# Top-k attention masks: one GpSimd pass per tile with byte output, in place of a split between VectorE and a two-pass GpSimd form

## The reference, cut to what matters

```python
q, kk, v = (proj(wq), proj(wk), proj(wv))           # 8 images x 8 heads, 3136 tokens, 8 values a head
scores = jnp.einsum('bhqd,bhkd->bhqk', q, kk) * scale
vals, idx = jax.lax.top_k(scores, k)                # k = 32 of 3136
w = jax.nn.softmax(vals, axis=-1)
vg = jnp.take_along_axis(v[:, :, None, :, :], idx[..., None], axis=3)
out = jnp.einsum('bhqk,bhqkd->bhqd', w, vg)
```

## Time and profile before

| | us |
|---|---|
| median of 3 runs | 40168.95 |
| lowest, highest | 40162.17, 40170.39 |
| the profiled execution | 40166.83 |
| its span, first to last instruction | 40165.2 |
| outside the span | 1.6 |

### The profile page before, as it was taken

One profiled execution on the slowest core, in us unless ns is written; L12 is line 12 of the kernel. 1 busy time (PEld: TensorE's weight loads), 2 busy tenths in 40 slices (PEclk: granted clock), 3 DMA queues, 4 the chain that ended last, 5 costly groups with the idle time before them and its releaser, 6 DMA issues. The chain is left out here.

```text
span 40165.2 us, 616606 instructions
## 1 busy us (share of the span) xinstructions
PE 27334.3 (68%) x190808; PEld 12487.9 (31%) x190809; DVE 34028.5 (85%) x144824; ACT 21387.4 (53%) x28193; POOL 23707.4 (59%) x9390
## 2 busy tenths in 40 slices
PE   4557676666767667767347677777776777674399
PEld 4533332222333323333123233333332333331122
DVE  5659999999999999999669999999999999996611
ACT  1126665555666656656146566666665666663111
POOL 0017776666867667867037677777776777773000
PEclk7778888888888888888578788888888888886555
DMA  0010000000000000000110000000000000001100
GB/s 36 8 51 5 5 5 5 4 4 4 5 5 5 5 4 5 5 5 5 51 50 5 4 5 5 5 5 5 5 5 4 5 5 5 4 5 42 55 10 6
DMA packets 133141, 454.41 MB, mean 11 GB/s; under 512 B 29244, under 2 KB 85444, under 8 KB 111240
## 3 DMA queue, kind: packets, MB, share of 16 engines
q1 hardware_dynamic: 129256, 410.72, 3.0%
HBM read 244.71 MB, written 165.93 MB: 10 GB/s over the span
## 5 line engine op out<-in xcount | busy, mean ns | idle before, releaser
L225 POOL TENSOR_SCALAR B<-S,M 128x3136 bf16<-128x3136 f32 (+1 forms) x1920 | 15768.6, 8213 | 7934.6 <-DVE M L525 7848.3
L493 DVE MAX8 C<-S 128x8 f32<-128x112 f32 x89600 | 18738.3, 263 | 1002.3 <-issue 751.5
L418 ACT COPY S<-banks 128x896 f32<-128x896 f32 (+1 forms) x12800 | 10210.9, 815 | 8585.1 <-DVE C L493 3667.1
L439 ACT ACTIVATE W<-banks 128x1024 f32<-128x1024 f32 (+1 forms) x9524 | 9735.7, 1023 | 2747.3 <-PE banks L333 2696.0
L324 PE MATMUL banks<-Q,K 99*128 99x512 bf16 (+2 forms) x22550 | 6836.4, 390 | 3341.2 <-ACT S L418 2742.3
L286 PE MATMUL banks<-K,Q 96*128 96x448 bf16 x22400 | 6852.1, 385 | 3128.3 <-ACT S L418 2747.0
L230 POOL CAST Z<-B 128x3136 fp8e4<-128x3136 bf16 (+1 forms) x1920 | 6704.5, 3492 | 380.9 <-PE banks L333 136.4
L333 PEld LDWEIGHTS banks<-NEG,Z 128*128 128x128 fp8e4 (+1 forms) x80450 | 5968.7, 105 | 2753.9 <-issue 823.1
L333 PE MATMUL banks<-NEG,Z 128*128 128x128 bf16 (+3 forms) x80450 | 6817.7, 230 | 0.0
L369 PE MATMUL banks<-W,V 128*32 128x512 f32 (+1 forms) x45100 | 6726.3, 577 | 109.2 <-ACT W L442 79.0
L535 DVE TENSOR_SCALAR Z<-S,M 128x3136 fp8e4<-128x3136 f32 x1280 | 6033.2, 4713 | 369.7 <-PE banks L333 369.6
(11 more groups left out here) (200 smaller groups left out, 21899.3 us busy)
## 6 DMA issues: line engine op xcount, KB each, us to landing
q<-ln_o SPq DMA_DIRECT2D x20, 1568.0 KB, 5.1
ln_x<-y SPq DMA_DIRECT2D x16, 1568.0 KB, 6.0
K<-k_parts SPq DMA_DIRECT2D x130, 147.0 KB
Q<-q_parts SPq DMA_DIRECT2D x130, 147.0 KB
q_parts<-pj_parts SPq DMA_DIRECT2D x24, 784.0 KB, 4.7
k_parts<-pj_parts SPq DMA_DIRECT2D x24, 784.0 KB, 7.8
V<-v_rows SPq DMA_DIRECT2D x130, 112.5 KB, 7.4
v_rows<-pj_vt SPq DMA_DIRECT2D x8, 1800.0 KB, 11.2
```

What stands on the lines that cost most here:

```text
L225: chained(lambda: pool.tensor_scalar(m.B[0:rows, :], m.S[0:rows, slot(tile), :], m.M8[0:rows, side(i), t, 31:32], None, ALU.is_lt))
L418: act.copy(m.S[0:rows, slot(tile), at:at + CW * w].rearrange("p (a n) -> p a n", a=w), m.AB[0:rows, pair(score_at[a]):pair(score_at[a]) + ...
L439: ins = act.activation(m.W[:, e % 4, 0:n_banks, :], m.AB[:, b:b + n_banks, :], ACT.Exp)
L493: ins = dve.max(m.C[0:rows, tile % 2, TOP_AT + k:RANKED:CHUNKS], m.S[0:rows, slot(tile), CHUNK * k:CHUNK * k + CHUNK])
```

## The change

All ten entries of `MAKERS` become P, so VectorE makes no masks. GpSimd makes each in one instruction, which has two arithmetic steps in place of one: compare, then multiply by `ONE` = 56.0. The output is written as unsigned bytes into `Z`: 56 is the bit pattern 0x38, which is 1.0 when TensorE reads the byte as `float8e4`. The scratch `B`, the cast, and the waits that tied the two passes and consecutive masks together go. The wait for the mask slot (`e_mm`), which stood between the passes, now stands ahead of the only one.

```diff
-MAKERS = "DPPDPDPPDP"
+MAKERS = "PPPPPPPPPP"
+ONE = 56.0
@@
                 pool.wait_ge(found, tile + 1)
-                masks_done = sum(maker(x) == "P" for x in range(tile))
-                if masks_done:
-                    pool.wait_ge(z_pool, masks_done)
-                chained(lambda: pool.tensor_scalar(m.B[0:rows, :], m.S[0:rows, slot(tile), :],
-                                                   m.M8[0:rows, side(i), t, 31:32], None, ALU.is_lt))
                 if mask_freed(tile):
                     pool.wait_ge(e_mm, mask_freed(tile))
-                pool.wait_ge(part, parts[0])
-                pool.tensor_copy(mask_at(tile)[0:rows, :], m.B[0:rows, :], saturate=False).then_inc(z_pool, 1)
+                pool.tensor_scalar(mask_at(tile)[0:rows, :].bitcast(U8), m.S[0:rows, slot(tile), :],
+                                   m.M8[0:rows, side(i), t, 31:32], ONE, ALU.is_lt, ALU.mult).then_inc(z_pool, 1)
```

More of the change, by code:

```diff
@@ L7 @@
 FP8 = mybir.dt.float8e4
+U8 = mybir.dt.uint8
 I32 = mybir.dt.int32
@@ L609, in attend_memory @@
             ("V1", [128, 2, NT, 32], F32), ("S", [128, RING, TOK], F32), ("Z", [128, MASKS - MAKERS.count("A"), TOK], FP8),
-            ("B", [128, TOK], BF16), ("W", [128, 4, 2, QW], F32), ("O4", [128, QW], F32), ("OS", [HD + 1, 2, QW], F32),
+            ("W", [128, 4, 2, QW], F32), ("O4", [128, QW], F32), ("OS", [HD + 1, 2, QW], F32),
             ("C", [128, 2, RANKED], F32), ("C8", [128, NT], F32), ("M8", [128, 2, NT, 32], F32),
```

## The result

| | before | after |
|---|---|---|
| median of 4 runs (us) | 40169.67 | 46847.24 |
| lowest, highest | 40162.17, 40172.84 | 46837.19, 46849.31 |
| the profiled execution, its span | 40166.83, 40165.2 | 46846.82, 46845.2 |

What follows compares the result with a forecast made beforehand. VectorE bounds the kernel now, GpSimd after the change. Attention goes from 32,125 to 27,672 + 286 (block turns) + 2309 (searches) = 30,267 us; with 14 more saved, 1872 off 40,166.8 gives 38,295 us, range 37,400 to 47,050.

Steps and rivals of the forecast that it cites:

- the first term of the sum: GpSimd's mask passes in attention: 3200 at 8.21 us; with small work 8.65 us a tile, 27,672 us for 128 heads.
- three units: GpSimd's old comparison: 2.548 ns an element, a unit being the plain pass's 0.8365 ns, or 2.62 us for 3136 elements.
- the searches: GpSimd standing while VectorE searches in attention: 23 us on 90 occasions plus 239 us for second searches, 2309 us together.
- groups of short work: GpSimd's shift instructions, seven groups a head, each 1.51 us from its start to the next mask, 10.6 us a head.
- the moved wait: GpSimd's wait for TensorE to free a mask slot, now ahead of the pass; cost at nothing with 23 us of cover.
- its pace without masks: VectorE in attention without its masks and the waits ahead of them: 9.115 - 2.07 = 7.04 us a tile.
- The rival on the other side: GpSimd's 3200 passes: the second step costs, 47,003 us at 11.01 us a pass, 46,450 with one more unit; 20 in 100.
- A GpSimd stop in a search: In a search GpSimd works for 8.21 + 1.51 us of the 32.0 and stands for 22.3.
- The argument of six masks against one set's fill: GpSimd has six masks, 52 us, before needing the slot, while TensorE needs 29 us to fill the set.
- the sign that GpSimd would wait nowhere for long for TensorE: Expected in the new trace's attention: TensorE's masks make GpSimd wait nowhere for long.
- The rival of a third of a unit: GpSimd's 3200 passes: the second step adds 0.87 us each, 41,000 us in all, slower by 2%; 12 in 100.
- The fast pass: GpSimd's pass falls below 6.8 us, TensorE and VectorE bound: 34,300 us, or 35,500 with bubbles of 5%; 11 in 100.

Runs made afterwards that it cites:

- one-step kernel: The changed kernel without the multiplication: all masks by GpSimd in one pass, comparison alone, byte output; 38507.06 us, 0.9584 of before.
- fast pair: The changed kernel with each GpSimd mask made by two fast passes, clamping to 0 or 255, then scaling 255 to 56; 33797.26 us, 0.8416 of before.

## Why the prediction was wrong

**The step that failed** is the first term of the sum, 3200 passes at 8.21 us. The prediction bounded the pass between 2.62 and 11.01 us and took the value of the old comparison, on the ground that "a body that already spends three units has room for one multiplication". It has not. The runs show that this second step costs one more unit of its own: 10.857 - 8.213 = 2.64 us, against the 2.62 of the unit in the earlier trace rows, with byte output and with bf16. The nearness of the row decided the choice, but that row had one step and the new pass two, and nothing in the rows spoke for a free one. Nearly the whole miss follows. By the prediction's own sum, 3200 x 2.64 less 90 x 2.64 inside the searches is 8,220 us, which makes 46,520; measured were 46,847, 8,552 above the forecast. Of the 330 us left, some 125 are the 896 groups of short work, each 1.65 us to the next mask and not 1.51. The rest wasn't taken apart in this kernel; the moved wait, below, is of that size in the one-step kernel.

Why a second step costs a unit, and why three pairs of steps are fast, no run here shows.

**What held.**

- VectorE was the bound, and its pace without masks is 7.04 us a tile: the fast pair ran at 7.06 in a stretch without a search.
- The one-step kernel tests all the rest of the sum with the pass that it assumed: 38,507 against 38,295. Two errors in it partly cancel: the moved wait (340 us too little), and the searches, where GpSimd mostly stood 21.5 to 21.9 us and 23 were taken (some 100 too much).
- The rival on the other side was right in mechanism and place, and within 1% in size. At its upper bound of 11.01 us it gave 47,003, with one whole unit 46,450; measured were 46,847 with a pass of 10.857. Its chance of 20 in 100 was too low: from 8.80 us on it is slower, and most of the stretch between the value taken and the upper bound lies beyond that.
- A GpSimd stop in a search: 32.0 us less the pass less 1.51. With 10.86 this is 19.6; the trace has 18.9.
- The range of 37,400 to 47,050 held the time, but it was so wide because two cases of opposite sign were in it. That says little for the forecast.

**What was off besides.** The moved wait has a price of some 340 us in the one-step kernel. The argument of six masks against one set's fill holds in the steady order; it does not hold at the start of a block and behind a search, where TensorE has not gone on. So the sign that GpSimd would wait nowhere for long for TensorE failed too. The old comparison takes its 8.21 us "whatever the other engines do" in the kernel before, but not in every order: with VectorE's masks beside it the one-step pass took up to 9.84 us.

The rival of a third of a unit is refuted: the step costs a whole unit, 2.64 us and not 0.87. The Trainium skill (GPSIMD Engine Reference, section 3.1) puts bodies of three or more operations at roughly three operations a cycle. If a multiplication is one operation, the trace does not agree with that.

The fast pass was a rival for the wrong reason: two steps can be fast, but in none of the forms tried with a comparison among them. The Trainium skill (GPSIMD Engine Reference, section 4.1) calls GpSimd roughly line-rate for one input. The trace agrees for multiply-add, 2.88 us against the 2.62 of the plain pass, and not for the forms of 8.2 and 10.86 us.

## What to carry to other kernels

A new form of an instruction on GpSimd, with one more arithmetic step or another operation, has no price until it is measured; 3136 columns took 2.88, 8.2 or 10.86 us by operation alone. When the sum turns on one unseen duration, compare it with the value at which nothing is won, and if the bounds reach far over that value, treat both sides as near even. Where an engine is to take over all of a kind of work, measure that one instruction first, on a scratch tile in the kernel before.

## What the runs showed of the hardware

- On GpSimd, a tensor-scalar instruction on 128 x 3136 floats takes 8.2 us with any single step tried (comparison, subtraction, maximum, multiplication) and 10.86 with most pairs of steps tried, but 2.88 when the pair is multiply-add, add-multiply or multiply-multiply. To multiply alone is thus dearer than to multiply and add nothing. With immediate numbers only, in place of the column, multiply-add took 2.81 us, the comparison 8.13 and its two-step form 10.78.
- Bytes, bf16 and float32 as output made no difference to the comparison, nor bytes and bf16 to its two-step form and to multiply-add. The mask of the fast pair rests on one thing more, that an overflow in the conversion to bytes clamps at 0 and 255; the output of that kernel comes out right, though no trace shows the bytes themselves.
- The VectorE mask took 1.85 us beside an idle GpSimd and on average 4.71, 6.24 and 6.75 us as GpSimd's longest instruction grew from 8.2 to 10.86 us and lost the short cast beside it. A mask that starts while a GpSimd instruction runs ends some 1.6 us behind the end of that instruction, so its mean duration belongs to what stands on GpSimd.
- TensorE's busy time a tile fell from 7.21 to 6.68 us between two stretches whose mean granted clock is 0.89 and 0.96 (1.0 being the upper level, 2.4 GHz). Taken as a fixed floor it was 500 us too high. The mean clock alone does not tell it: the stretch of the changed kernel has 626.34 / 87.8 = 7.14 us a tile at 0.80. What else sets it stays open.
